# Split-operand q/k projections in two causal attention stages, and a reordered gated linear attention stage

## The reference

```python
# layer 0 on LN(x): 4 heads, 32 channels of q and k and 64 of v per head
q, k, v = x @ Wq.T, x @ Wk.T, x @ Wv.T             # q times 128 ** -0.5
g = log_sigmoid(x @ Wgk1.T @ Wgk2.T + bgk2) / 32   # log decay per channel
# per head: S_t = diag(exp(g_t)) S_{t-1} + k_t v_t^T ;  o_t = q_t^T S_t
# o: RMS norm per head and token, times silu(x @ Wg.T), then @ Wout.T ; x = x + that
# layers 2 and 4 on LN(x): 16 heads of 8 channels
q, k, v = h @ Wq + bq, h @ Wk + bk, h @ Wv + bv    # layer 2: W = A[h] @ B[h]; layer 4: W = tanh(sub . Wl) * W0 + B0
o = softmax(where(causal, q k^T / sqrt(8), -inf)) v
x = x + o @ Wo + bo
```

## Time and profile before

| | |
|---|---|
| median of 3 runs | 1880.42 us (1876.57 to 1883.0) |
| profiled execution | 1879.84 us, span 1878.1 us |
| mean granted clock of PE | 0.877 |
| stage 0 | 0 to 210 us |
| stage 2, stage 4 with its feed-forward part | from 345 us to 583 us, from 780 us on |
| q and k projections (L1676) | 64, in 128 MATMUL instructions |

### The profile page before, as it was taken

One profiled execution on the slowest core, in us unless ns is written; L12 is line 12 of the kernel. 1 busy time (PEld: TensorE's weight loads), 2 busy tenths in 40 slices (PEclk: granted clock), 3 DMA queues, 4 the chain that ended last, 5 costly groups with the idle time before them and its releaser, 6 DMA issues. The chain is left out here.

```text
span 1878.1 us, 25330 instructions
## 1 busy us (share of the span) xinstructions
PE 1521.0 (81%) x9201; PEld 930.5 (50%) x9222; DVE 1163.2 (62%) x2854; ACT 823.7 (44%) x1277; POOL 798.2 (42%) x835
## 2 busy tenths in 40 slices
PE   3677588899997999659998788979999999984094
PEld 2455455644444677424444567755554544533063
DVE  5656688568884775667885333257877778755002
ACT  4553244236664644425665343245545455430041
POOL 5441344512224855522223353335545556452633
PEclk8787699759997999857999889989999999996597
DMA  2000000100000000300000000000000000005123
GB/s 76 1 2 2 30 1 1 77 1 1 1 1 22 1 1 1 127 1 1 1 2 1 16 32 1 1 1 1 1 1 1 1 1 1 1 0 191 56 57 91
DMA packets 20827, 37.59 MB, mean 20 GB/s; under 512 B 1760, under 2 KB 18144, under 8 KB 19552
## 3 DMA queue, kind: packets, MB, share of 16 engines
q1 hardware_dynamic: 18656, 31.76, 4.9%
q0 software_dynamic: 2048, 4.21, 0.7%
HBM read 26.50 MB, written 9.47 MB: 19 GB/s over the span
## 5 line engine op out<-in xcount | busy, mean ns | idle before, releaser
L1859 DVE CUSTOM_DVE_ANT_0 s_masked_scores<-s_for_max,s_mask_qk 128x128 bf16<-128x128 f32 (+3 forms) x512 | 227.5, 487 | 63.4 <-PE s_for_max L1695 59.9
L2246 POOL TENSOR_TENSOR wbuf<-s_probs 128x1024 f32<-128x1024 f32 x64 | 152.1, 2377 | 206.9 <-ACT s_probs L2405 206.8
L1651 POOL TENSOR_SCALAR_AFFINE_SELECT s_probs<-s_probs 128x256 f32<-128x256 f32 x256 | 101.1, 408 | 312.3 <-ACT s_probs L1796 246.5
L2405 ACT ACTIVATE s_probs<-s_scores 128x1024 f32<-128x1024 f32 x128 | 132.3, 1034 | 201.8 <-PE s_scores L2327 201.8
L1140 POOL TENSOR_TENSOR s_hidden_lo<-s_hidden,s_hidden_hi 128x512 fp32r<-128x512 f32 x108 | 142.5, 1320 | 119.4 <-ACT s_hidden_hi L1251 119.2
L2447 DVE TENSOR_REDUCE s_negmax<-s_for_max 128x2 f32<-128x1024 f32 x126 | 152.1, 1207 | 21.2 <-PE s_for_max L2302 21.2
L1695 PE MATMUL s_for_max<-s_k_stack,s_q_stack 32*128 32x128 f32 (+3 forms) x512 | 137.9, 442 | 33.1 <-DVE s_max_wide L1859 26.8
L1695 PEld LDWEIGHTS s_for_max<-s_k_stack,s_q_stack 32*128 32x128 f32 x512 | 69.3, 205 | 169.5 <-DVE s_max_wide L1859 113.9
L2454 DVE RECIPROCAL s_recip<-s_pv_and_sums 128x128 f32<-128x128 f32 x128 | 116.7, 934 | 47.1 <-PE s_pv_and_sums L2353 47.1
L1796 ACT ACTIVATE s_probs<-s_scores 128x1024 f32<-128x1024 f32 x128 | 126.8, 1023 | 21.8 <-PE s_scores L1716 18.2
L2340 PE MATMUL s_pv_and_sums<-s_probs,s_v 128*64 128x512 f32 x512 | 123.9, 605 | 0.9 <-DVE wbuf L2462 0.9
(11 more groups left out here) (449 smaller groups left out, 3696.9 us busy)
## 6 DMA issues: line engine op xcount, KB each, us to landing
s_w<-extra SPq DMA_DIRECT2D x2, 2048.0 KB, 10.2
wbuf<-w SPq DMA_DIRECT2D x1, 3460.0 KB, 10.8
s_probs<-extra SPq DMA_DIRECT2D x1, 2898.0 KB, 9.6
wbuf<-w SPq DMA_DIRECT2D x1, 2888.0 KB, 14.6
wbuf<-w SPq DMA_DIRECT2D x1, 2124.0 KB, 8.4
dispatched<-s_empty_slots SPq DMA_DIRECT2D x1, 2064.0 KB, 16.6
s_rows<-dispatched SPq DMA_DIRECT2D x8, 258.0 KB
expert_rows<-s_empty_slots SPq DMA_DIRECT2D x1, 2048.0 KB, 22.1
```

The lines of the kernel that those rows point to most:

```text
L1651: last = nc.gpsimd.affine_select(out=diag, in_=diag, compare_op=ALU.is_ge, fill=0.0, base=0, pattern=[[0, diag.shape[1]], [1, P]], channel ...
L1859: last = nc.vector.tensor_tensor_reduce(out=junk[:, m % 2, at:at + n], in0=p1[m % 2][:, at:at + n], in1=mask[:, S - n:S], scale=1.0, scala ...
L2246: nc.gpsimd.tensor_tensor(added[half], probs[:, g % 2, 2 * half, :, :], probs[:, g % 2, 2 * half + 1, :, :], ALU.add).then_inc(s_added, 1)
L2405: nc.scalar.activation(probs[:, g % 2, j, :, :], p2[:, :, :], ACT.Exp, scale=dh ** -0.5).then_inc(s_exp, 1)
```

## The change

**Stage 0.** The four ACT copies of each `qx` become four DMAs on SP of 32x512 from `qT` (64 KB each), behind the load of the next stage's weights (3460 KB) on that queue. `project` runs gk, q, z, k in place of gk, q, k, z. `values(0)` moves from the first loop turn to a place before `sums(0)`, with the DVE and ACT parts moved accordingly; `sums(1)` moves behind `within(0, ...)`. The output part of the last sequence runs in two halves of 256 tokens. **Stages 2 and 4.** LN output and stacked weights are held as a hi and a lo part in fp32r, and a projection is three fp32r matmuls. DVE makes the lo weights and the first sequence's lo part, POOL the other three.

```diff
@@ stage 0 @@
-            return [(m, c) for m in ("gk", "q", "k", "z")]
-        jobs += project_jobs(0) + [("b", 0)] + project_jobs(1) + [("b", 1)]
+            return [(m, c) for m in ("gk", "q", "z", "k")]
+        jobs += project_jobs(0) + [("vg", 0, i) for i in range(TPC)] + [("b", 0)] + project_jobs(1)
...
         def _(sp):
             sh.load_next(sp, stage)
+            for c in range(B):
+                if c < 2:
+                    sp.wait_ge(s_cleared, c + 1)
+                sp.wait_ge(s_qk, 2 * c + 1)
+                for h in range(heads):
+                    rows = slice(h * dk, (h + 1) * dk)
+                    sp.dma_start(qx[rows, c % 2, h, :], qT[rows, c % 2, :]).then_inc(s_qx[c % 2], 16)
...
+            def rms_half(k):
+                pool.wait_ge(s_ss, B + k)
...
+                nc.gpsimd.tensor_tensor(rrms[:, part(k)], ss[:, part(k)], sh.mhalf[:, part(k)], ALU.pow).then_inc(s_rms, 1)
...
             ln.turned(pe, 1)
-            pe.wait_ge(s_const, 6)
+            values(0)
+            pe.wait_ge(s_const, 5)
             sums(0)
...
-            turn_o(B - 1)
-            project_out(B - 1)
+            for k in range(2):
+                turn_half(k)
+                project_half(k)
...
             def _(act):
...
-                for h in range(heads):
-                    rows = slice(h * dk, (h + 1) * dk)
-                    nc.scalar.activation(qx[rows, c % 2, h, :], odd_bank("q", c)[rows, :], ACT.Copy,
-                                         scale=dk ** -0.5).then_inc(s_qx, 1)
...
-                mean_square(c)
-            gated(B - 1)
-            residual(B - 1)
+                if c + 1 < B:
+                    mean_square(c)
+                else:
+                    mean_square_half(0)
+                    mean_square_half(1)
+            gated_half(0)
+            gated_half(1)
+            residual_half(0)
+            residual_half(1)
@@ stages 2 and 4 @@
+        pool.wait_ge(ln.s_lo, 1)
+        for c in range(1, B):
+            ln.low_part_by(nc.gpsimd, pool, c)
...
-            nc.tensor.matmul(pm[:, :], wst["qk".index(what)][:, g * P:(g + 1) * P], sh.xnT[:, c * S:(c + 1) * S],
-                             start=True, stop=True).then_inc(s_proj, 1)
+            pe.wait_ge(ln.s_lo, c + 1)
+            (w_hi, w_lo), at, cs = wst["qk".index(what)], slice(g * P, (g + 1) * P), slice(c * S, (c + 1) * S)
+            nc.tensor.matmul(pm[:, :], w_hi[:, at], ln.hi[:, cs], start=True, stop=False)
+            nc.tensor.matmul(pm[:, :], w_lo[:, at], ln.hi[:, cs], start=False, stop=False)
+            nc.tensor.matmul(pm[:, :], w_hi[:, at], ln.lo[:, cs], start=False, stop=True).then_inc(s_proj, 1)
...
         before_vector(dve)
+        ln.low_part(dve, 0)
...
-        ln = LayerNorm(sh, ctx, tag, p1)
+        ln = LayerNorm(sh, ctx, tag, p1, split=True)
...
+            for k in range(2):
+                dve.wait_ge(s_whi, k + 1)
+                nc.vector.tensor_tensor(wst[1][:, k, :, 0:3, :],
+                                        p2[k][:, 0:D].rearrange("p (h d) -> p h d", h=H8).unsqueeze(2).broadcast_to(
+                                            [P, H8, 3, HD8]),
+                                        wst[0][:, k, :, 0:3, :].bitcast(F32), ALU.subtract).then_inc(s_wlo, 1)
```

More of the change, by code:

```diff
@@ L232, in copied @@
         dst, ps = self.sh.xnT[:, c * S:(c + 1) * S], self.ps[c % 2][:, :] if ps is None else ps
-        if self.split:
+        if self.split and self.affine:
+            nc.scalar.activation(self.hi[:, c * S:(c + 1) * S], ps, ACT.Identity, bias=self.affine[1],
+                                 scale=self.affine[0]).then_inc(self.s_hi, 1)
+        elif self.split:
             nc.scalar.copy(self.hi[:, c * S:(c + 1) * S], ps).then_inc(self.s_hi, 1)
@@ L404, in gated_linear_attention @@
                 jobs.append(("y", c - 1))
-            else:
-                jobs += [("vg", 0, i) for i in range(TPC)]
             if c + 1 < B:
@@ L424, in emptied @@
             if what in "qk":
[L425 to L426 removed]
+                return [(s_qk, 2 * c + "qk".index(what) + 1)]
+            return [({"gk": s_gk, "z": s_z, "b": s_bs, "kd": s_kd, "y": s_x}[what], c + 1 + sum(job[2:]))]
         block = ctx.enter_context(nc.Block())
@@ L506, in project @@
                 nc.tensor.matmul(ps[0:rank, :], w["wgk1"], xc, start=True, stop=True).then_inc(s_proj, 1)
-                for name in "qk":
-                    ps = take(name, c)
-                    nc.tensor.matmul(ps, w["w" + name], xc, start=True, stop=True).then_inc(s_proj, 1)
+                ps = take("q", c)
+                nc.tensor.matmul(ps, w["wq"], xc, start=True, stop=True).then_inc(s_proj, 1)
                 ps = take("z", c)
@@ L515, in project @@
                 last.then_inc(s_zp, 1)
+                ps = take("k", c)
+                nc.tensor.matmul(ps, w["wk"], xc, start=True, stop=True).then_inc(s_proj, 1)
             def sums(c):
@@ L632, in project_out, with turn_half, project_half @@
                 last.then_inc(s_y, 1)
+            def turn_half(k):
+                pe.wait_ge(s_og, B + k)
+                for i in range(TPC)[two(k)]:
+                    for n in range(2):
+                        last = nc.tensor.transpose(ps_a[:, n, i * P:(i + 1) * P], og[:, i, n * P:(n + 1) * P], sh.ident[:, :])
+                last.then_inc(s_ogT, 1)
+            def project_half(k):
+                ps = take("y", B - 1, k)
+                pe.wait_ge(s_ogTs, 2 * (B + k))
+                for i in range(TPC)[two(k)]:
+                    for n in range(2):
+                        last = nc.tensor.matmul(ps[:, i * P:(i + 1) * P], ogT[:, n, i * P:(i + 1) * P],
+                                                w["wout"][:, n * D:(n + 1) * D], start=(i % 2 == 0 and n == 0),
+                                                stop=(n == 1), skip_group_check=True)
+                last.then_inc(s_y, 1)
             ln.turned(pe, 0)
@@ L649, in _ @@
                     within(c, m)
+                if c == 0:
+                    sums(1)
                 if c + 2 < B:
@@ L761, in _ @@
             softplus(0)
+            gates(0)
             sums(0)
@@ L787, in _ @@
                 windows(c)
-                if not c:
-                    gates(0)
                 if c + 1 < B:
@@ L795, in _ @@
                 squares(c, 1)
-            turned_o(B - 1)
+            for k in range(2):
+                turned_half(k)
         @block.vector
@@ L1924, in weights_vector @@
             dve.wait_ge(sh.wsem[stage], 16)
+            for k in range(2):
+                dve.wait_ge(s_whi, k + 1)
[3 more added lines that the diff above has]
+                                        wst[0][:, k, :, 0:3, :].bitcast(F32), ALU.subtract).then_inc(s_wlo, 1)
         def norm_gpsimd(pool):
-            nc.gpsimd.memset(wst[:, :, :, 3, :], 0.0).then_inc(s_zero, 1)
+            for part in wst:
+                nc.gpsimd.memset(part[:, :, :, 3, :].bitcast(F32), 0.0).then_inc(s_zero, 1)
             ln.gpsimd(pool)
@@ L2010, in generated_attention @@
         ca, cab = gen["ca_w"], gen["ca_b"]
-        stacked = [wst[:, k, :, :, :].rearrange("p h r d -> p (h r d)") for k in range(2)]
+        stacked = [[part[:, k, :, :, :].rearrange("p h r d -> p (h r d)") for part in wst] for k in range(2)]
         causal_attention(sh, stage, ctx, ln, probs, p1, p2, po, pm, stacked, cab[:, 0:2 * QUADS], s_wst,
```

121 lines of the change are left out of this document (81 added, 40 removed).

## The result

Median 1870.47 us over 10 runs (1865.05 to 1874.17), before 1879.17 over 10 runs (1874.58 to 1885.59). The ratio is 0.9948, 95% interval 0.9933 to 0.9963: 8.7 us faster by the medians, 9.8 by the ratio, about half of the forecast 19. One of the four executions of experiment 10 was in a slow state (2523.9 us, granted clock 0.544), and that experiment's ratio is of the other three. The profiled execution of the changed kernel took 1869.46 us, with a span of 1867.7; the one of before took 1879.84 with 1878.1.

The account below looks back on a forecast made before the run. Stage 0 was taken as a chain of waits, the causal stages as PE-bound with DVE close behind when warm. Terms -8.6 + 5.4 - 8.1 - 7.7 = -19.0 against 1879.84 gave 1861 us, range 1853 to 1872.

Parts of the forecast that it names:

- rival A: Causal stages: DVE takes over as bound, warm gain is nothing and the head costs 8; 1871 us, chance 0.12.
- the late rise: Cold head of causal stages: clock rises one quad later, some 6 us, alone giving 1867; chance 0.06.
- rival B: Stage 0: later sums push the second sequence's chain as much as the turn saves, only tail stays; 1865, chance 0.17.
- Head and values of stage 0: Stage 0: first loop turn gains 4.6 us, later first sums cost 2.5; net gain 2.1, bounds 0 to 5.6.
- Turn 1: Stage 0, loop turn 1: PE's wait for ACT before z goes, as the copies are gone; -2.4 us.
- Turns 2 and 3: Stage 0, loop turns 2 and 3: nothing counted, since PE waits for DVE's late normalization anyway.
- rival D: Stage 0: the block DMAs land late for three of four sequences; +11 us at most, 1872, chance 0.04.
- Tail: Stage 0, end: output of the last sequence in halves gains 4.1 us, bounds 3 and 5.
- Heads of the causal stages: Stages 2 and 4, start: DVE's added differences delay its bias steps, 2.2 and 3.2 us; +5.4, bounds 3.4 and 8.
- Cold projections: Stages 2 and 4, slow clock: each projection 0.58 us shorter, 7 counted per stage; -8.1 us in all.
- Warm projections: Stages 2 and 4, fast clock: 0.32 us less per quad, 12 quads per stage; -7.7 us, bounds 0 and 13.
- Rival C: Warm quads: shorter projections let PE's clock fall, 2.9 us each, 7 falls eating 19 us; chance 0.06, late rise another 0.06.

Follow-up runs that it names:

- experiment 10: Changed kernel with sums(1) back in place, POOL's bias additions behind DVE's setup steps, and four delaying DVE memsets before stage 2 and 4 LN: 1866.98 us, ratio 0.9943.
- Experiment 3: Changed kernel with the second sequence's sums, and the steps hanging on them, back at their former place: 1864.53 us, ratio 0.9914 to before.
- Experiment 4: Changed kernel with POOL's four output-bias additions made to wait until after DVE's setup steps: 1861.40 us, ratio 0.9893 to before.
- experiment 2: Kernel before with only the causal stages' part of the change, stage 0 left as it was: 1876.40 us, ratio 0.9978.

## Why the prediction came out as it did

**The number.** The miss of 8.6 us is made of stage 0 (1.5), the heads (2.2), the cold and warm quads (2.5 together), the fall (4.0) and the stages' ends (1.4), less 3.0 in stages that the change does not touch. Of the cases that lay above the forecast, rival A and the late rise did not happen and rival B did in part; the range held by its width and by those 3.0 us.

**What bounds what.** Right. In the cold part PE sets the pace, in the warm part the time taken out of PE came back quad by quad, and DVE did not take over (rival A): 10.36 us for 10.67, and 10.13 with two products.

**Head and values of stage 0.** The forecast was -2.1 us at the start of L540; measured +1.1. The sums of sequence 0 start at 34.62 us, 35.5 was forecast. The step that failed is the sentence on the first loop turn, where "the later sums shift DVE's chain by about 2.5": it priced the shift of the first sequence's sums only. The second sequence's, which the diff moves behind the within products, went from 49.67 to 62.77 us, and with them POOL's exponents, ACT's factors and DVE's scaled products. Experiment 3 prices that at 5.4 us at this place. Without it the head is 4.3 us shorter than before, about the 4.6 of the sum. It is rival B in part, by a cause that rival B did not name.

**Loop turns.** Turn 1: -3.3 for -2.4. Turns 2 and 3 up to the last state product: -1.2 for 0. **The DMAs** land in 2.1 us and nobody waits for them; rival D is out. **Tail**: -3.8 for -4.1.

**Heads of the causal stages.** +7.6 for +5.4. The mechanism was right, the term too small. I had 1.1 us for the lo part and 1.0 for the weights, and in stage 4, where POOL works beside all of them, they take 1.74 and 2.64. Experiment 4 shows that 6.2 us of it is POOL's contention; 1.5 stay without it.

**Cold projections.** -6.9 for -8.1. I took start to start of consecutive passes, 0.58 us of difference. What counts here is the end of the last pass, which ACT waits for: before 2.12 us (368.18 to 370.30), now 1.69 (365.12 to 366.81), 0.43 less. Over 7 projections in two stages that is 6.0 us. The other 0.9 comes from the clock: in stage 4 the last cold quad is 1.8 us shorter (14.00 for 15.80) and not 0.9, since PEclk rises earlier in it.

**Warm projections.** 0.30 per quad for 0.32, as forecast. From a q projection to the k projection it is 3.04 us for 3.28, from there to the next q projection 7.32 for 7.38: 0.24 and 0.06, where 0.27 and 0.05 were forecast. But only 0.16 of the 0.24 lies in the q projection (0.89 to 0.90 us up to the next product in most quads, for 1.05; 0.78 was forecast); the rest is that the k projection follows the product ahead of it 0.09 earlier (0.41 for 0.50 us). That the two together gave the forecast 0.27 nearly is luck. Of the two ways to price the three passes the row was nearer. The Trainium skill, "TensorE: Matmul & The Clock Gate", "Back-to-back issue gap", gives 131 ns as sustained spacing of 512-column matmuls; successive passes here start 0.24 us apart (446.55 and 446.79), which does not bear that figure out and is nearer to its isolated 216 ns.

**Rival C, the clock.** It was given 0.06 with falls, on the other side. It is what takes most of the rest: 4.0 us in the changed kernel's execution, 10.5 in that of experiment 2. Its point of decision, seven falls, was not reached with three products; with two it was (8 quads, 23 us, in the slowest execution). Its other half, a later rise of the clock, did not happen: PEclk rose earlier in both cold parts. The argument against it, that "the three passes keep PE active in the same places", failed. That falls of PEclk last longer when the projections are shorter is what the traces show (3.4 us, 6.8 to 10.2, up to 13.7). That they come more often rests on one execution with two products against eight with three; four products had three falls, f32 one per execution. Which quads they hit changed from trace to trace, with the start of the stage or just with the execution: the runs do not tell these apart. The f32 kernels' falls cost only 1.5 us each because they are short. Why they are short, and why PEclk fell at all with PE busy all along, stays open. The same page of the Trainium skill, section "HAM oscillation — how this bites in real kernels", explains repeated falls by pauses of PE for DMAs; here PE is busy for 94% of the ten us ahead of the fall and waits for no DMA, so these rows show falls which that account does not cover.

**Other stages.** -3.0 us in stages that the change leaves alone; their PEclk levels differ in place between the executions, stage 3 by -1.8, stage 1 by +1.1, and what follows stage 4 by -2.3. I do not count this as an effect of the change.
